# Splitting GpSimd's two-head additions into one instruction per head, in an attention and feed-forward block

## The reference

```python
x = L0_attn_x                                          # [1, 2048, 128]
qkv = _layernorm(x) @ w_qkv                            # 16 heads x 64, three times
sim = jnp.einsum('bhid,bhjd->bhij', q, k) * 64 ** -0.5
attn = jax.nn.softmax(sim, axis=-1)
out = jnp.einsum('bhij,bhjd->bhid', attn, v)
x = x + out.reshape(1, 2048, 1024) @ w_out + b_out
gate, y = fp4_linear(_layernorm(x), w_gate), fp4_linear(_layernorm(x), w_up)
x = x + fp4_linear(silu(gate) * y, w_down)             # hidden width 352
```

## Time and profile before

| what | value |
|---|---|
| median of 3 runs | 1327.34 us (1326.15 to 1327.88) |
| the profiled execution's own time | 1330.24 us |
| its span, first to last instruction | 1328.4 us |
| mean granted TensorE clock | 0.982 |
| TensorE busy | 1256.3 us (95%) |
| VectorE busy | 910.3 us (69%) |
| ScalarE busy | 882.3 us (66%) |
| GpSimd busy | 1036.6 us (78%) |

### The profile page before, as it was taken

One profiled execution on the slowest core, in us unless ns is written; L12 is line 12 of the kernel. 1 busy time (PEld: TensorE's weight loads), 2 busy tenths in 40 slices (PEclk: granted clock), 3 DMA queues, 4 the chain that ended last, 5 costly groups with the idle time before them and its releaser, 6 DMA issues.

```text
span 1328.4 us, 24703 instructions
## 1 busy us (share of the span) xinstructions
PE 1256.3 (95%) x7405; PEld 664.9 (50%) x7405; DVE 910.3 (69%) x2386; ACT 882.3 (66%) x1244; POOL 1036.6 (78%) x464
## 2 busy tenths in 40 slices
PE   4999999999999999999999999999999999798676
PEld 3555555555455555555455555555545544444335
DVE  6766767677666666667666666666766667778788
ACT  5767676677666767667667767677767667564443
POOL 4488888988888888888788888898888887876333
PEclk9999999999999999999999999999999999999888
DMA  2000000000000000000000000000000000000001
GB/s 64 2 10 1 1 2 10 1 1 2 3 10 1 1 2 10 1 2 2 3 10 1 1 2 10 1 2 2 1 3 1 1 2 1 1 1 1 0 1 33
DMA packets 45953, 6.68 MB, mean 5 GB/s; under 512 B 37344, under 2 KB 45664, under 8 KB 45808
## 3 DMA queue, kind: packets, MB, share of 16 engines
q1 hardware_dynamic: 45584, 4.41, 2.6%
q0 software_dynamic: 224, 0.54, 0.1%
HBM read 3.75 MB, written 1.05 MB: 4 GB/s over the span
## 4 chain that ended last, share of the span: by engine, by line
PE 84%; DVE 8%; issue 6%; ACT 1%; POOL 1%; DMA 0%; POOLq 0%; SPq 0%; DVEq 0%; ACTq 0%
PE o_ps L1273 32%; PE s_ps L1114 25%; PE mx_ps L1136 8%; PE mx_ps L1129 4%; PE misc_ps L1263 3%; PE misc_ps L1251 2%; PE misc_ps L1101 2%; PE misc_ps L1079 2%; PE s_ps L1122 1%; PE misc_ps L1081 1%; PE misc_ps L1080 1%; PE s_ps L1360 1%; DVE scaled L801 1%; DVE split L798 1%; DVE amax L823 1%
## 5 line engine op out<-in xcount | busy, mean ns | idle before, releaser
L567 POOL TENSOR_TENSOR acc_pool<-acc_pool,probs 128x1024 f32<-128x1024 f32 x343 | 829.6, 2419 | 50.7 <-POOL acc_pool L567 40.4
L685 ACT ACTIVATE probs<-s_ps 128x1024 f32<-128x1024 f32 x512 | 524.9, 1026 | 67.2 <-PE s_ps L1114 44.0
L862 DVE CUSTOM_DVE_ANT_0 summed<-mx_ps,rise 128x512 bf16<-128x512 f32 x503 | 344.6, 685 | 281.4 <-issue 237.4
L1273 PE MATMUL o_ps<-probs,vv 128*64 128x512 f32 x2048 | 495.5, 604 | 0.1
L605 ACT ACTIVATE rise<-mx_ps 128x512 f32<-128x512 f32 x503 | 300.1, 597 | 277.5 <-PE mx_ps L1129 269.5
L1273 PEld LDWEIGHTS o_ps<-probs,vv 128*64 128x64 f32 x2048 | 127.2, 136 | 222.5 <-issue 182.6
L1136 PE MATMUL mx_ps<-k_hi,q_hi 64*128 64x512 f32 x503 | 223.4, 444 | 14.0 <-issue 9.3
L1129 PE MATMUL mx_ps<-k_raw,q_hi 64*128 64x512 f32 x503 | 224.3, 446 | 7.4 <-DVE part_max L862 7.4
L1114 PE MATMUL s_ps<-q_hi,k_hi 64*128 64x512 f32 x1024 | 207.3, 396 | 0.0
L1114 PE MATMUL s_ps<-q_hi,k_lo 64*128 64x512 f32 x1024 | 205.8, 393 | 0.0
L1114 PE MATMUL s_ps<-q_lo,k_hi 64*128 64x512 f32 x1024 | 205.1, 392 | 0.0
(11 more groups left out here) (176 smaller groups left out, 1102.7 us busy)
## 6 DMA issues: line engine op xcount, KB each, us to landing
mrow<-neg_max SPq DMA_DIRECT2D x256, 0.5 KB, 2.0
wqkv<-in_L_attn_w_qkv SPq DMA_DIRECT2D x8, 192.0 KB, 2.9
y<-in_L_attn_x SPq DMA_DIRECT2D x4, 256.0 KB, 4.2
out<-y SPq DMA_DIRECT2D x4, 256.0 KB, 2.6
wo<-in_L_attn_w_out SPq DMA_DIRECT2D x8, 64.0 KB, 1.9
wx<-in_L_ffn_w_down POOLq DMA_DIRECT2D x1, 176.0 KB, 5.9
wx<-in_L_ffn_w_gate POOLq DMA_DIRECT2D x1, 128.0 KB, 4.7
wx<-in_L_ffn_w_up POOLq DMA_DIRECT2D x1, 128.0 KB, 5.7
```

Source lines behind the costliest of these rows:

```text
L567: pool.tensor_tensor(acc, first, probs[:, j % P_BUFS, :, :], ALU.add) \
L685: act.activation(probs[:, j % P_BUFS, :, :], s_ps[:, j % 2, :, :], ACT.Exp, scale=SCALE) \
L862: dve.tensor_tensor_reduce(summed[:, s % 2, :], mx_bank(h, pair), rise[:, h, :], 1.0, LOWEST, ALU.add, ALU.max, part_max[:, slot:slot + 1] ...
L1273: ins = pe.matmul(o_ps[DH * h:DH * (h + 1), :], vv[par(w)][:, j, DH * h:DH * (h + 1)], probs[:, j % P_BUFS, h, :], start=(j == 0), stop=(j ...
```

## The change

Each addition of GpSimd in the attention units, 128 partitions by two heads of 512, becomes two instructions of 128x512, head 0 and then head 1. The waits in front of an addition stand once, ahead of the first half; the semaphore is raised once, by the second half. No wait stands between the halves, which touch different columns. This holds for the additions of exponentials in all 32 units and for the combining additions. Nothing else is changed: the other engines' instructions and waits are the same.

```diff
                         first = probs[:, 0, :, :] if k == 0 else acc
-                        pool.tensor_tensor(acc, first, probs[:, j % P_BUFS, :, :], ALU.add) \
+                        pool.tensor_tensor(acc[:, 0, :], first[:, 0, :], probs[:, j % P_BUFS, 0, :], ALU.add)
+                        pool.tensor_tensor(acc[:, 1, :], first[:, 1, :], probs[:, j % P_BUFS, 1, :], ALU.add) \
                             .then_inc(pool_adds, 1)
...
-                        pool.tensor_tensor(acc, acc, acc_dve[:, w % 2, :, :], ALU.add).then_inc(den_acc, 1)
+                        other = acc_dve[:, w % 2, :, :]
+                        pool.tensor_tensor(acc[:, 0, :], acc[:, 0, :], other[:, 0, :], ALU.add)
+                        pool.tensor_tensor(acc[:, 1, :], acc[:, 1, :], other[:, 1, :], ALU.add).then_inc(den_acc, 1)
```

## The result

The changed kernel takes 1333.06 us (1331.73 to 1334.96, 6 runs) against 1327.37 us (1326.15 to 1329.45, 6 runs). The ratio is 1.0042, with a 95% interval of 1.0031 to 1.0052: slower by 5.7 us. The profiled execution took 1334.96 us, its span is 1333.1 us, 4.7 us longer than the span before.

What follows compares the result with a forecast made beforehand. TensorE's 36.76 us per unit was taken as the bound, in slow units a GpSimd-VectorE ring. Own time 1330.24 + 3 - 2 = 1331.2, less 2.9 from profiled run to median, gave 1328.3 us; range 1323 to 1340.

Steps and rivals of the forecast that it cites:

- The bound before: Attention units before the change: TensorE's own work of 36.76 us, in slow units a GpSimd-VectorE ring of 37.02 us.
- the price of a pair: Each GpSimd addition: two halves take 2.52 us against 2.39 us whole, 0.13 us more.
- the ring after: GpSimd and VectorE waiting on each other in a changed unit: 37.1 us, from 36.9 to 37.3.
- the +3: Loop units: of +6 us over 25 units, half reaches TensorE, since GpSimd regains time at loop borders.
- rival A: Second halves dearer than in the prologue, GpSimd bounds every unit: 1341 us at 0.17 per pair, 1368 at 0.25; chance 0.18.
- The ring before: Unit 14 before the change: GpSimd's 33.32 us of work plus 3.70 us waiting for VectorE, 37.02 us.
- How much of it TensorE sees: Exponential 0's slack just fits; GpSimd's regained time spares three or four units of eight after each loop border: +3 us.
- The end: Units 28 to 31: shorter VectorE waits behind halves outweigh longer final additions, -2 us, between -4 and +1.
- Rival B: Loop units: VectorE waits for both queued halves, TensorE's next unit 1.4 us late in half of 25; 1345 us, chance 0.06.
- Rival C: Loop units: shorter lock waits put the ring below TensorE's 36.76 us, gaining 2.3 us plus 2 at the end; 1323, chance 0.16.

Runs made afterwards that it cites:

- e7: Kernel before, with each GpSimd addition of 128x1024 made into four instructions of 128x256; 1451.70 us, ratio 1.0931.
- e1: Kernel before, with only GpSimd's first six additions of each unit split into halves, none in unit 31; 1350.44 us, ratio 1.0168.
- e8: Kernel before, with only the last GpSimd addition of exponentials in each unit split; 1331.36 us, ratio 1.0024.
- e4: Kernel before, nothing split; in units 0 to 27 GpSimd does one addition less and VectorE one more; 1325.94 us, ratio 0.9989.
- e2: Kernel before, with only additions 7 to 12 of each unit split, the combining one whole; 1327.27 us, ratio 0.9994.
- e3: Kernel before, no addition split; a small 128x4 GpSimd addition on a scratch tile put in front of each of the 406 additions; 1344.88 us, ratio 1.0133.
- e6: Kernel before, with additions split only in units 28 to 31, the combining ones too; 1329.96 us, ratio 1.0011.
- e9: Kernel before, with only additions 9 to 12 of units 0 to 27 split, the combining ones whole; 1329.06 us, ratio 1.0013.

## Why the prediction was right, and where its terms were off

The time was in the range of 1323 to 1340, and on the slower side, to which the prediction gave 0.39 against 0.45 for no change. It lies 1.1 us above the band of the forecast itself (1325 to 1332), and the sum of 1328.3 was 4.8 us low. Where these come from: 3.1 from unit 28 on (-2 predicted, +1.1 on TensorE), 0.3 in front of unit 0, 0.3 in units 0 to 27 (+3 predicted, +3.3 measured), and 1.0 from the step from the profiled execution to the median (2.9 us before, 1.9 in the changed kernel). The bound before, the price of a pair and the ring after were right; the +3 came out by luck, as two of its terms were wrong in opposite directions. Step by step:

- **The price of a pair.** 0.13 us from the prologue. In the units the undisturbed halves take 1.27 to 1.30 us and start 1.24 or 1.25 us apart. Right, so rival A is out; e7 shows the same part of a start for 128x256.
- **The ring before.** 37.02 us in unit 14; in state W from one combining addition to the next it is 36.85 to 37.02 from unit to unit, with TensorE's 36.76 beside it. e1 (+0.8 us in that ring gives +0.82 per unit) and e8 (+0.13 gives +0.14) show that it decides, and e4 that all units take 36.76 once it is cleared. That 36.76 is TensorE's own work held: e2 and e4 have it in nearly all units on TensorE. But the 2.3 us that the prediction shared out over 25 units are not all the ring's: 1.1 of them are unit 16 (37.86 us), where the granted clock was at 0.50 (1.2 GHz) for 3.4 us from 641.0 on.
- **The ring after.** Predicted 37.1, from 36.9 to 37.3, measured 37.01, with `o_norm` at the gap (0.26 us) and L1020 at the gap (0.78 us). L1020 got in ahead of addition 12, as the step said. The reason that I gave for it in the sum, that VectorE no longer waits for a whole addition, was wrong: e3 shows the same with whole additions. What does it is that thirteen pairs make GpSimd 1.6 us late. `o_norm` (0.96 instead of 2.42 us) is shorter in e3 too (1.13 us in the mean), so that isn't the halves' doing either.
- **How much of it TensorE sees.** Predicted: half of 25 units, +3 us. Measured: exponential 0 starts 0.03 us after GpSimd's last addition in all of units 1 to 23 but 8 and 16, at 0.14 us more per unit on TensorE, +2.9 in the 21 units and +0.3 at the borders. A shorter ring, touched more often. The sum came out right by that; the part of it that said three or four units of eight are spared was wrong. Only units 8 and 16 were (36.72 and 36.76 us on TensorE), and units 24 to 27, for another reason, the shorter gaps behind the loop.
- **Unit 0** looks like a step that was left out: from its exponential 0 to the next it is 1.4 us longer. On TensorE it is 0.1 us. The other 1.3 are exponential 0 of unit 1, which had time to spare and now waits for GpSimd (1.15 us of idle).
- **The end** is the term that was mis-sized. Predicted -2 us for unit 28 and everything behind it; measured -0.4 by the exponentials and +1.1 on TensorE: -2.9 in unit 31 and behind it, but +4.0 in units 28 to 30 (+2.6 by the exponentials), whose longer additions I had called hidden. The saving that the -2 was made of did not come. The four operations of the earlier trace rows were to be 1.2 us shorter, twice, and are 0.24 us shorter in unit 29 and 0.05 in unit 30; VectorE's waits there hardly shrink with the halves (below, unit 29 in the changed kernel). The shorter end comes from elsewhere, and e6 leaves open whether by the granted clock.

```profile
1158.77 4.98 DVE L788 TENSOR_SCALAR fx<-y,mv,root 128x128 f32<-128x128 f32 x4 [4.26 <-POOL root L539]
```

- **Rival B** (issue order decides between queued halves) fell in e2: an operation issued during the first half ran before the second, as the earlier trace rows had it. The changed kernel shows the same where L1023 meets the halves, and no L1023 of the loop takes over the 2.4 us that B needed (2.19 at most). By the sentence of the Trainium skill that the prediction quotes (SBUF — State Buffer, section "Who interferes with whom"), read as it reads it there, the second half would have gone first; the measurement decides. **Rival C** needed units of 36.76 throughout and didn't come.

## What to carry to other kernels

Two engines that exclude each other form a ring with each other's waits, and its length depends on the order in which they meet as much as on the work. So six splits in a unit cost 23 us or nothing, by their place, and making one engine later can shorten the ring. Idle in front of an instruction is slack only as far as it doesn't consist of the other engine's work behind one's own last instruction; take that off first. And a stretch between two instructions of an engine that waits is no measure of the engine that bounds: cut the span on the bounding engine as well, or a shift is read as a loss (unit 0) or as a gain (the 36.63 us of e2).

## What the runs showed of the hardware that I had not expected

- The ring has two states, and small shifts decide which one holds: a VectorE addition issued 0.05 us after a GpSimd addition began waited for all of it (3.41 us in e3), one issued 0.4 us before the gap's end got in (1.34 us). In e9 the states mostly alternate from unit to unit, 37.44 and 36.20 us.
- GpSimd's idle in front of an addition that reads the one before is 0.16 us in the hardware loop (units 0 to 23) and 0.08 us in the straight code behind it, in both kernels and in e3. That is 1 us per unit, where the ring of unit 14 was 0.26 us longer than TensorE's 36.76.
- What is saved can be less than nothing at first: 0.13 us more in one addition of a unit (e8) cost 3.6 us over the kernel, 1.7 us more per unit (the change) only 5.7.
